# Attention scores contracted over each head's own 32 rows, heads issued in alternating pairs, with the normaliser worked out per half batch and the masked copies of q dropped

## The reference, cut to what matters

```
qh = q.reshape(Bq, Sq, nh, dh).transpose(0, 2, 1, 3)
kh = k.reshape(Bq, Sq, nh, dh).transpose(0, 2, 1, 3)
vh = v.reshape(Bq, Sq, nh, dh).transpose(0, 2, 1, 3)
...
log_D = jnp.where(ltr, log_fg_mat + ig[:, :, None, :], -jnp.inf)
max_log_D = jnp.max(log_D, axis=-1, keepdims=True)
D = jnp.exp(log_D - max_log_D)
qk = jnp.einsum('bhsd,bhtd->bhst', qh, kh) / jnp.sqrt(jnp.float32(dh))
C = qk * D
normalizer = jnp.maximum(jnp.abs(jnp.sum(C, axis=-1, keepdims=True)), jnp.exp(-max_log_D))
h = jnp.einsum('bhst,bhtd->bhsd', C / (normalizer + EPS_BACKEND), vh)
mean = jnp.mean(h, axis=-1, keepdims=True)
var = jnp.var(h, axis=-1, keepdims=True)
h_norm = (h - mean) / jnp.sqrt(var + EPS_NORM)
```

## Time and profile before

| | |
|---|---|
| median of three runs | 2007.04 us (2004.08 to 2008.09) |
| the profiled execution's own time | 2012.26 us |
| its span in the trace | 2010.5 us |
| TensorE busy, matmuls | 1664.2 us (83%) |
| VectorE, ScalarE, GpSimd busy | 1276.8, 451.6, 558.8 us |
| attention loop in the trace | 63.1 to 175.9 us |

### The profile page before, as it was taken

One profiled execution on the slowest core, in us unless ns is written; L12 is line 12 of the kernel. 1 busy time (PEld: TensorE's weight loads), 2 busy tenths in 40 slices (PEclk: granted clock), 3 DMA queues, 4 the chain that ended last, 5 costly groups with the idle time before them and its releaser, 6 DMA issues.

```text
span 2010.5 us, 28661 instructions
## 1 busy us (share of the span) xinstructions
PE 1664.2 (83%) x9489; PEld 1427.3 (71%) x9490; DVE 1276.8 (64%) x2539; ACT 451.6 (22%) x751; POOL 558.8 (28%) x423
## 2 busy tenths in 40 slices
PE   4798536767887007687999999999999999999998
PEld 4796425326877006575888888888888888888887
DVE  3453579784555574656676767676767676767675
ACT  2443020212333002222111211121112111211111
POOL 1234224854760766462010101010101010101010
PEclk9897757978999558797999999999999999999999
DMA  9100001314765320000000000000000000000001
GB/s 361 38 1 11 16 0 53 107 55 135 221 216 158 94 73 27 11 32 16 17 31 16 31 16 31 16 31 16 31 16 31 16 31 16 31 16 31 16 0 42
DMA packets 54064, 106.00 MB, mean 53 GB/s; under 512 B 6513, under 2 KB 37809, under 8 KB 54001
## 3 DMA queue, kind: packets, MB, share of 16 engines
q1 hardware_dynamic: 21744, 63.21, 9.2%
q10 hardware_dynamic: 26112, 25.17, 4.0%
q0 software_dynamic: 6144, 16.79, 2.6%
HBM read 69.50 MB, written 35.65 MB: 52 GB/s over the span
## 4 chain that ended last, share of the span: by engine, by line
PE 75%; DVE 11%; POOL 4%; issue 4%; DMA 3%; ACT 2%; SPq 1%; POOLq 0%; DVEq 0%; ACTq 0%
PE ps L1409 37%; PE ps L1425 20%; PE ps L1503 3%; DMA xl<-slots_in 2%; POOL yg L1237 2%; PE ps L1463 2%; PE ps L1302 2%; PE ps L1522 1%; DVE xn L424 1%; DVE hH L577 1%; PE ps L1483 1%; POOL hL L1194 1%; DVE st L433 1%; PE ps L1358 1%; PE ps L1303 1%
## 5 line engine op out<-in xcount | busy, mean ns | idle before, releaser
L1409 PE MATMUL ps<-xTH,wH 128*128 128x512 f32 x1088 | 429.2, 395 | 7.8 <-POOL wL L1189 5.9
L1409 PE MATMUL ps<-xTH,wL 128*128 128x512 f32 x1088 | 428.5, 394 | 0.0
L1409 PE MATMUL ps<-xTL,wH 128*128 128x512 f32 x1088 | 425.0, 391 | 0.0
L1189 POOL TENSOR_TENSOR wL<-wS,wH 128x1536 fp32r<-128x1536 f32 (+1 forms) x36 | 122.6, 3406 | 913.2 <-ACT wH L980 913.2
L845 DVE TENSOR_TENSOR hF<-sg,ps 128x512 f32<-128x512 f32 x256 | 175.8, 687 | 306.2 <-ACT sg L985 306.1
L985 ACT ACTIVATE sg<-ps 128x512 f32<-128x512 f32 x264 | 157.6, 597 | 905.4 <-PE ps L1409 905.4
L1425 PE MATMUL ps<-wH,hH 128*128 128x256 f32 x1152 | 327.9, 285 | 16.2 <-POOL hL L1194 15.6
L1425 PE MATMUL ps<-wL,hH 128*128 128x256 f32 x1152 | 327.0, 284 | 0.0
L1425 PE MATMUL ps<-wH,hL 128*128 128x256 f32 x1152 | 326.9, 284 | 0.0
L854 DVE TENSOR_TENSOR hL<-hF,hH 128x512 fp32r<-128x512 f32 x256 | 258.4, 1010 | 0.1
L1425 PEld LDWEIGHTS ps<-wH,hH 128*128 128x128 f32 x1152 | 220.8, 192 | 35.0 <-POOL hL L1194 23.7
(11 more groups left out here) (298 smaller groups left out, 2323.0 us busy)
## 6 DMA issues: line engine op xcount, KB each, us to landing
wS<-in_w SPq DMA_DIRECT2D x32, 768.0 KB, 4.4
slots_in<-qM SPq DMA_DIRECT2D x16, 768.0 KB, 13.9
eS<-in_wr SPq DMA_DIRECT2D x32, 384.0 KB, 3.7
xl<-slots_in ACTq DMA_DIRECT2D x48, 256.0 KB, 3.4
slots_out<-yo ACTq DMA_DIRECT2D x48, 256.0 KB, 3.6
x<-in_x SPq DMA_DIRECT2D x1, 2048.0 KB, 8.8
cx<-in_ctx SPq DMA_DIRECT2D x1, 2048.0 KB, 14.4
wS<-in_wab SPq DMA_DIRECT2D x4, 512.0 KB, 4.4
```

The costliest lines, as they stand in the source:

```text
L1189: pool.tensor_tensor(blocks(wL, slot, plain), blocks(wS, slot, plain), f32(blocks(wH, slot, plain)), ALU.subtract).then_inc(w_low, 1)
L1409: last = pe.matmul(ps[:, 2 * half + b, :], piece(w, s, slot, col, P), v[:, k, g * 512:(g + 1) * 512], start=q == 0, stop=q == 5)
```

## The change

The matmuls of the scores read `kT` and `qT` directly, each over its head's own 32 rows, so `qM`, GpSimd's copies and the semaphore `q_masked` go (the buffer stays, since a DMA reads zeros from it). `scores` is now called for two heads at once and alternates between them, first the 256-column matmul of each, then the 128-column matmul of each. The two heads stand on different groups of 32 rows. The decays are a function of their own. PSUM is dealt out anew: four banks for scores, two for decays, and two for outputs, one for each half of a batch's heads (four heads). `Cm` has four buffers. VectorE's normaliser and scaling run twice per batch, each time for four heads; means and variances stay once per batch.

```
-        Cm = at("Cm", [P, 3, 384], F32, end["Dm"])
+        Cm = at("Cm", [P, 4, 384], F32, end["Dm"])
...
+            def half_out(b, half):
+                hs = slice(4 * half, 4 * half + 4)
+                o = ps[:, 6 + half, 0:8 * (DH + 1)].rearrange("p (s h d) -> p s h d", s=2, h=4)
+                v = hN[:, b % 2, :].rearrange("p (s h d) -> p s h d", s=2, h=NH)[:, :, hs, :]
+                dn = den[:, :, hs]
+                dve.wait_ge(pv_done, 8 * b + 4 * half + 4)
+                link(dve.tensor_copy(dn, o[:, :, :, DH]))
+                link(dve.scalar_tensor_tensor(dn, dn, -1.0, dn, ALU.mult, ALU.max))
+                link(dve.tensor_tensor(dn, dn, eE[:, :, 8 * b + 4 * half:8 * b + 4 * half + 4], ALU.max))
+                link(dve.tensor_scalar(dn, dn, 1e-6, None, ALU.add))
+                link(dve.reciprocal(dn, dn))
+                wait(dve, head_centred, b - 1)
+                dve.tensor_tensor(v, o[:, :, :, 0:DH], dn.unsqueeze(3).to_broadcast([P, 2, 4, DH]), ALU.mult).then_inc(head_read, 1)
...
-                wait(dve, pv_done, i - 2)
-                dve.scalar_tensor_tensor(Cm[:, i % 3, :], ps[:, i % 2, 0:384], float(DH) ** -0.5, Dm[:, i % 2, :],
+                wait(dve, pv_done, i - 3)
+                dve.scalar_tensor_tensor(Cm[:, i % 4, :], ps[:, i % 4, 0:384], float(DH) ** -0.5, Dm[:, i % 2, :],
                                          ALU.mult, ALU.mult).then_inc(mixed_done, 1)
-                if i >= 8 and i % 8 in (2, 3, 4, 7):
-                    head_work(i // 8 - 1, (2, 3, 4, 7).index(i % 8))
+                if i % 8 == 6:
+                    half_out(i // 8, 0)
+                if i >= 8 and i % 8 == 2:
+                    half_out(i // 8 - 1, 1)
...
-            def mask_queries(heads):
-                for i in heads:
-                    if i < B * NH:
-                        r, c, t0 = DH * (i % 4), i % NH // 4, i // NH * SEQ
-                        wait(pool, qk_done, i - 11)
-                        pool.tensor_copy(qM[r:r + DH, i % 12, :], qT[r:r + DH, c, t0:t0 + SEQ]).then_inc(q_masked, 1)
-                        pool.wait_ge(q_masked, i + 1)
...
-                wait(pe, mixed_done, i - 1)
-                pe.wait_ge(q_masked, i + 1)
-                pe.matmul(ps[:, i % 2, 0:256], kT[:, c, t0:t0 + P], qM[:, i % 12, :], start=True, stop=True)
-                pe.matmul(ps[:, i % 2, 256:384], kT[:, c, t0 + P:t0 + SEQ], qM[:, i % 12, P:],
-                          start=True, stop=True).then_inc(qk_done, 1)
+                wait(pe, mixed_done, i - 2)
+                for part in range(2):
+                    first = part * P
+                    for j in range(2):
+                        r, c = DH * ((h + j) % 4), (h + j) // 4
+                        last = pe.matmul(ps[:, (i + j) % 4, 2 * first:2 * first + SEQ - first], kT[r:r + DH, c, t0 + first:t0 + first + P],
+                                         qT[r:r + DH, c, t0 + first:t0 + SEQ], start=True, stop=True)
+                        if part == 1:
+                            last.then_inc(qk_done, 1)
...
-            for i in range(B * NH):
+            for i in range(0, B * NH, 2):
                 scores(i)
+                decays(i)
                 if i >= 2:
                     values(i - 2)
+                decays(i + 1)
+                if i >= 2:
+                    values(i - 1)
```

More of the change, by code:

```diff
@@ L232, in build @@
         rowsT_copied = sem("rowsT_copied")
-        q_masked = sem("q_masked")
         qk_done = sem("qk_done")
@@ L488, in _ @@
             dve.tensor_copy(MHL[64:, :], r2[0:64, :]).then_inc(rows_done, 1)
[L490 to L497, removed]
@@ L499, in head_work @@
-            def head_work(b, part):
-                o = ps[:, 4 + 2 * (b % 2):6 + 2 * (b % 2), 0:NH * (DH + 1)].rearrange("p s (h d) -> p s h d", h=NH)
-                v = hN[:, b % 2, :].rearrange("p (s h d) -> p s h d", s=2, h=NH)
[L503 to L517, removed]
@@ new lines, in head_mean, with head_variance @@
+            def head_mean(b):
+                v = hN[:, b % 2, :].rearrange("p (s h d) -> p s h d", s=2, h=NH)
+                dve.wait_ge(head_read, 2 * b + 2)
+                link(dve.tensor_reduce(mean[:, b % 2, :, :], v, AXX, ALU.add))
+                dve.tensor_scalar(mean[:, b % 2, :, :], mean[:, b % 2, :, :], 1.0 / DH, None, ALU.mult).then_inc(head_scaled, 1)
+            def head_variance(b):
+                dve.wait_ge(head_squared, b + 1)
+                q = hQ[:, b % 2, :].rearrange("p (s h d) -> p s h d", s=2, h=NH)
+                link(dve.tensor_reduce(var[:, b, :, :], q, AXX, ALU.add))
+                dve.tensor_scalar(var[:, b, :, :], var[:, b, :, :], 1.0 / DH, EPS, ALU.mult, ALU.add).then_inc(head_var, 1)
@@ L521, in _ @@
                 dve.wait_ge(decay_done, i + 1)
-                wait(dve, pv_done, i - 2)
-                dve.scalar_tensor_tensor(Cm[:, i % 3, :], ps[:, i % 2, 0:384], float(DH) ** -0.5, Dm[:, i % 2, :],
+                wait(dve, pv_done, i - 3)
+                dve.scalar_tensor_tensor(Cm[:, i % 4, :], ps[:, i % 4, 0:384], float(DH) ** -0.5, Dm[:, i % 2, :],
                                          ALU.mult, ALU.mult).then_inc(mixed_done, 1)
-                if i >= 8 and i % 8 in (2, 3, 4, 7):
-                    head_work(i // 8 - 1, (2, 3, 4, 7).index(i % 8))
-            for part in range(4):
-                head_work(B - 1, part)
+                if i % 8 == 6:
+                    half_out(i // 8, 0)
+                if i >= 8 and i % 8 == 2:
+                    half_out(i // 8 - 1, 1)
+                if i >= 8 and i % 8 == 4:
+                    head_mean(i // 8 - 1)
+                if i >= 8 and i % 8 == 7:
+                    head_variance(i // 8 - 1)
+            half_out(B - 1, 1)
+            head_mean(B - 1)
+            head_variance(B - 1)
             dve.wait_ge(const_loaded, 13 * 16)
@@ L929, in _ @@
                 wait(act, mixed_done, i - 1)
-                act.activation(Dm[:, i % 2, 0:256], ps[:, 2 + i % 2, 0:256], ACT.Exp, bias=aT[:, 0, i:i + 1])
-                act.activation(Dm[:, i % 2, 256:384], ps[:, 2 + i % 2, 256:384], ACT.Exp, bias=aT[:, 1, i:i + 1]).then_inc(decay_done, 1)
+                act.activation(Dm[:, i % 2, 0:256], ps[:, 4 + i % 2, 0:256], ACT.Exp, bias=aT[:, 0, i:i + 1])
+                act.activation(Dm[:, i % 2, 256:384], ps[:, 4 + i % 2, 256:384], ACT.Exp, bias=aT[:, 1, i:i + 1]).then_inc(decay_done, 1)
                 if i >= 8 and i % 8 == 6:
@@ L1155, in rows_of @@
                 return ap.rearrange("p s h -> p (s h)").unsqueeze(2).to_broadcast([P, 2 * NH, DH])
-            mask_queries(range(10))
             for b in range(B):
-                mask_queries(range(8 * b + 10, 8 * b + 18))
                 hc = hC[:, b, :].rearrange("p (g d) -> p g d", d=DH)
@@ L1297, in scores, with decays @@
                 b, h = i // NH, i % NH
-                c = h // 4
                 t0 = b * SEQ
-                wait(pe, mixed_done, i - 1)
-                pe.wait_ge(q_masked, i + 1)
-                pe.matmul(ps[:, i % 2, 0:256], kT[:, c, t0:t0 + P], qM[:, i % 12, :], start=True, stop=True)
-                pe.matmul(ps[:, i % 2, 256:384], kT[:, c, t0 + P:t0 + SEQ], qM[:, i % 12, P:],
-                          start=True, stop=True).then_inc(qk_done, 1)
+                wait(pe, mixed_done, i - 2)
[7 more added lines that the diff above has]
+                            last.then_inc(qk_done, 1)
+            def decays(i):
                 wait(pe, decay_done, i - 1)
-                pe.matmul(ps[:, 2 + i % 2, 0:384], idb[:, :], maskT[:, :], start=True, stop=False, skip_group_check=True)
-                pe.matmul(ps[:, 2 + i % 2, 0:256], sel[:, i, :], MHL[:, :], start=False, stop=False, skip_group_check=True)
-                pe.matmul(ps[:, 2 + i % 2, 256:384], sel[:, i, :], MHL[:, P:SEQ], start=False, stop=True,
+                pe.matmul(ps[:, 4 + i % 2, 0:384], idb[:, :], maskT[:, :], start=True, stop=False, skip_group_check=True)
+                pe.matmul(ps[:, 4 + i % 2, 0:256], sel[:, i, :], MHL[:, :], start=False, stop=False, skip_group_check=True)
+                pe.matmul(ps[:, 4 + i % 2, 256:384], sel[:, i, :], MHL[:, P:SEQ], start=False, stop=True,
                           skip_group_check=True).then_inc(arg_done, 1)
@@ L1313, in values @@
                 b, h = i // NH, i % NH
-                o0, o1 = (ps[:, 4 + 2 * (b % 2) + s, h * (DH + 1):(h + 1) * (DH + 1)] for s in range(2))
+                o0, o1 = (ps[:, 6 + h // 4, (4 * s + h % 4) * (DH + 1):(4 * s + h % 4 + 1) * (DH + 1)] for s in range(2))
                 pe.wait_ge(mixed_done, i + 1)
[L1316 to L1320, removed]
-            for i in range(B * NH):
+                if h % 4 == 0:
+                    wait(pe, head_read, i // 4 - 1)
+                pe.matmul(o0, Cm[:, i % 4, 0:P], vext[:, 2 * b, h, :], start=True, stop=True)
```

(9 more changed lines are left out.)

## The result

The changed kernel takes 2065.65 us (median of 4 runs, 2064.2 to 2071.86) against 2006.18 us (2004.08 to 2008.09): ratio 1.0303, 95% interval 1.0279 to 1.0326, so 59.5 us slower. Forecast was 2080 us, 72.8 us slower. The profiled execution took 2065.33 us, with a span of 2063.2 us.

What follows compares the result with a forecast made beforehand. TensorE was taken to bound the loop, at the lower clock throughout: scores 1.70, decays 1.30, values 2.20 and row-count changes 0.60 make 5.80 us a pair, 72.8 us more over 32 pairs, 2080 us; range 2035 to 2119.

Steps and rivals of the forecast that it cites:

- The clock stays down: Loop: PEclk stays at 0.50 from its start to its end, because part of the work uses few rows; chance 0.78.
- the rival of the drains: Rival from the experiments, given no chance: changes of row count, which stop TensorE for a moment, keep the clock down.
- Scores of a pair, and the changes of row count: Loop, per pair at the lower clock: partly overlapping scores 1.70 us (ends 1.28 and 2.55), two row-count changes 0.60 us.
- Values at 1.2 GHz: Loop's values at the lower clock: 1.1 us a head, 2.2 a pair; ends 0.64 and 1.28 a head.
- Decays: Loop's decays at the lower clock: 0.65 us a head, 1.30 a pair, unchanged.
- Sum: Whole loop: 5.80 us a pair, 32 pairs 185.6 us against 112.8, so 72.8 us slower.
- Edits at nothing: Normaliser, moved waits and L1335 hidden behind other work; last scaling gains at most 0.3 us; all taken at nothing.
- The Trainium skill: Two rules: matmuls on different 32-row groups overlap (scores 1.70, else 2.55 us); activity raises the clock, which the prediction doubted.
- The first rival: Loop: clock rises as before and heads overlap, 3.12 us a pair against 3.42, 9.6 us faster, 1997 us; chance 0.10.

Runs made afterwards that it cites:

- rows128: Changed kernel with its pairs, banks and half-batch normaliser, but scores over all 128 rows against GpSimd's masked q; 2070.76 us against 2078.70 for the kernel before, ratio 0.9954.
- rows32_only: Kernel before with one edit: each head's scores contract over its own 32 rows, heads one by one; 2186.23 us against 2078.70.
- changes_cold: Kernel before plus one small matmul over 32 rows and 8 columns ahead of every second head's scores; 2092.14 us against 2078.95.
- rows32_warm: Kernel before with each head's scores over its own 32 rows, plus 23 matmuls over 128 rows ahead of the loop; 2183.52 us.
- warm: Changed kernel plus 23 matmuls over 128 rows into a free bank ahead of the loop; 2053.95 us against 2078.70 for the kernel before, ratio 0.9875.
- not_alternated: Changed kernel with both score matmuls of the first head issued ahead of both of the second's; 2132.59 us against 2133.01 for the changed kernel.
- before_again: Kernel before, unchanged, run again for its trace on a later chip; 2077.14 us.

## Why the prediction was right, point by point

- **The clock stays down.** Right, and now shown: rows128 and rows32_only split the change, and changes_cold takes the rival of the drains away. That few rows count for less held in both directions, but for the fall it is rows32_warm that shows it, and not L1335, which the prediction read it from: in warm the clock fell 0.8 us before the 64-row matmuls began, behind a wait of TensorE in the last values, so what L1335 had to do with the fall in the kernel before is open. What the prediction did not see is that the loop would keep the clock if it had it: warm does, up to its last values.
- **Scores of a pair, and the changes of row count.** Mis-sized: 1.70 + 0.60 = 2.30 us expected, 1.58 + (1.36 - 1.24) = 1.70 measured. The overlap was right but its model wrong: the prediction let each record start behind the one ahead in the program, when in fact the heads run wholly side by side, the lower end given (1.28), and the order of issue does not matter (not_alternated). Of the rest, at most 0.42 us go to the two changes, 0.30 within the scores (1.58 - 1.28) and 0.12 behind the values (1.36 - 1.24), where 0.60 were taken; and some 0.1 of that need be no change, since a head's scores over whole rows take 1.38 and not 1.28 at this clock (66.63 - 65.25). Idle time of the weight loads, forecast at both changes, shows at one only, ahead of L1307.
- **Values at 1.2 GHz.** Mis-sized: 1.1 us a head taken, 1.24 measured, near the doubling that was the upper end (1.28). The ratio of the loads' durations, 1.73, was the wrong guide; the spacing of the loads goes from 0.107 to 1.24 / 6 = 0.21 us.
- **Decays.** 0.65 taken, 0.62 measured.
- **Sum.** 5.42 in place of 5.80 us a pair, 32 x 0.38 = 12 us of loop, 60.8 in place of 72.8. The medians differ by 59.5. That the forecast came this near is in part luck: scores and changes were 0.60 us a pair too dear and the decays 0.06, the values 0.28 too cheap, and these errors cancel in part.
- **Edits at nothing.** Right. The last scaling shrank, rows128 shows no cost of the normaliser, and L1339 ended under ScalarE's chain as said, though it took 5.67 us and not 5.1.
- **The Trainium skill.** Its rule in "TensorE: Matmul & The Clock Gate", Part 3, that matmuls at different groups of 32 rows run concurrently, is what the traces show, here for float32 too. The rule of Part 1, activity releases the throttle, is too coarse for this loop: 173.44 busy of 173.60 us, and 0.50.
- **The first rival** (clock up, heads overlapping) was priced at 3.12 us a pair; warm made it real at 2.92. The scores came at the 0.86 us of their eight weight loads, as priced; the changes were priced at 0.30 and took some 0.1 (2.92 - 0.86 - 1.96).

## What to carry to other kernels

Contracting over a head's own rows is worth something only with TensorE's clock in hand, and it can cost that clock: before cutting a matmul to few rows, look at where the granted clock stands when the stretch begins, and what runs on whole rows around it. If the stretch follows a pause, matmuls over all rows into a free bank during that pause can cost nothing, as here, and decide it (the loop went from 173.9 to 95.0 us, the time from 2133.01 to 2053.95, on two chips on which the kernel before differs by 0.25). That an engine is busy for all of a stretch does not tell its clock; read that row first.

## What the runs showed of the hardware that was not expected

- Float32 matmuls of two heads on different groups of 32 rows overlap in full: eight records in 1.58 us at 1.2 GHz, where one head's four alone take 1.57, and 0.86 at 2.4. At 1.2 GHz the order of issue made no difference (1.59 us).
- The same loop stays at 0.50 for all of its 173.6 us if it starts there, and at 1.00 from 62.5 to 156.9 us if it starts there.
- On two chips the profile shows pauses with no wait between the float matmuls of one stage (starts 2.80 us apart in before_again), and the kernel before and the changed one took some 70 us longer there than on the first chip.
